# A new order of tasks within a pair, on all five queues of an attention and channel-mix kernel

## The chip, the cores and the metric

The kernel runs on one core of one Trainium2 chip. The metric is device time in microseconds, from launch to end, as the median of several executions. The core has TensorE (PE; its weight loads are listed as PEld), VectorE (DVE), ScalarE (ACT), GpSimd (POOL) and a sync queue (SP) that issues DMAs. Each of them works through its own list of instructions in order, and they meet at semaphores.

## What is computed

One transformer-like layer on x of 8 x 1024 x 256, with 16 heads of 64:

```
h   = layernorm(x)
q,k,v = h @ Wq, h @ Wk, h @ Wv                     # per head, 64 wide
s   = q k^T / 8 + bias[clip(j - i + 16, 0, 32)]    # causal
a   = softmax(s) @ v                               # 16 heads side by side: 1024
x2  = x + layernorm(a @ Wp + bp)
n   = layernorm(x2);  p = n shifted down by one token
r   = sigmoid((mu_r n + (1 - mu_r) p) @ W_r^T)
k   = relu((mu_k n + (1 - mu_k) p) @ W_k^T)^2
out = x2 + layernorm(r * (k @ W_v^T))
```

## The kernel before

**Tiling.** The unit of work is a pair: two heads of one batch element, 8 x 8 = 64 pairs, n = 0 to 63 (n = 2m + par, so par is 0 in an even pair, and `at` is n mod 8). While attention runs for pair n, the second pass over the row maxima ("next") is made for pair n+1, q, k and v are projected ("qkv") for pair n+2, the block of 128 tokens n+10 is loaded, normalised and transposed ("xt"), and the tail of the layer runs for older blocks: the output projection ("proj") for block n-8, the mix ("mix") for n-9, the last matmul and gate ("ffn") for n-10. Not all parts run in all pairs: "xt" up to n = 53, "proj" from 8, "mix" from 9, "ffn" from 10. The tails of the last eight blocks are done after the last pair, in code of its own.

**Numbers as a pair of fp16.** Matmul operands are split: a high part (fp16 copy, made by ACT) and a low part (difference, made by VectorE or GpSimd), and three products are summed. So nearly each result of TensorE in PSUM is read first by ACT and then by VectorE before its bank is free.

**The tasks of a pair.** Attention of a pair goes through 12 tiles of scores (`TILES`), keys by queries, up to 128 x 512 for both heads. `score(t)` writes one of two score banks, `add_bias` (VectorE) adds the position bias to tiles on the diagonal, `exponential` and `high_probs` (ACT) follow, then `low_probs` on VectorE, or on GpSimd for tiles 4, 6, 7, 8, 10. Score t needs the bank of score t-2, that is low part t-2, or exponential t-2 for a tile of GpSimd, which copies out to SBUF. `weigh_values(k)`, k = 0 to 3 (tasks o0 to o3), multiplies probabilities and values of two blocks of 128 tokens; 2 and 3 of a pair run in the next pair. `outputs(k)` divides by the sums, into o_stage, and `store_chunk` writes o_stage to o_scratch in DRAM, in two halves. `fill(0)` to `fill(8)` write raw scores of the next pair to max_ps and `maxima` (VectorE) reduces them; `transpose_maxima(0)` and `(1)` turn the results over, also in max_ps, ACT's `shift` scales them to shift_row, and the sync queue's `load_shift` spreads them to shift_all, which enters the scores as one more product (L633). fill(0) waits for shift 1, because it writes what shift 1 reads; score 4 waits for the second half of shift_all.

**Banks.** All other tasks of TensorE share two PSUM banks, misc0 and misc1. The list `TASKS` gives their order in a pair, with the bank of each. `opened` (L551) lets a task wait until the task before it on the same bank is freed by its last reader (`freed`, L343). The order is written out by hand once for each engine, in `body` of each block, and must agree with `TASKS`.

**The sync queue.** `held` makes it wait for a semaphore, and everything behind it waits too. load_outputs (o_cur, 512 KB, for the output projection) waits until all chunks it reads are stored; load_head (xh, 128 KB) for the last transpose of a block; load_values (v_pair, 516 KB) for the values of a block of heads, which par 1 asks for in the pair in which the last of them, v1, is projected; load_residual (x_res, 128 KB) for GpSimd's last residual; store_out for GpSimd's `final`.

**GpSimd.** `head`, `residual_norm`, `final` and `residual` are layer norms (`normalise`, L382 to L399, a chain of tiny steps and one of 256 columns), each behind VectorE's `statistics`.

**The lists.** The old order of TensorE in a pair is: ffn, fill 0, score 1, o2, q0, q1, fill 1, scores 2 and 3, o0, o3, ot0, score 4, fill 2, o1, ot1, fill 3, scores 5 and 6, k0, first transpose of the maxima, k1, fill 4, scores 7 and 8, fill 5, v0, fill 6, score 9, x2t, proj, fill 7, score 10, xt, v1, fill 8, rk, score 11, score 0 of the next pair, second transpose of the maxima.

## Time and profile before

| | us |
|---|---|
| median of 3 executions (2397.15 to 2404.86) | 2400.41 |
| profiled execution | 2395.8 |
| its span, first to last instruction | 2394.0 |
| TensorE busy | 2221.1 |
| VectorE busy | 2043.0 |
| ACT busy | 1681.4 |
| GpSimd busy | 1498.1 |

The busy times are of the whole span. A pair takes some 35 us; the first 80 us go to loads and to the splitting of the weights, and the last 100 us to the tails of the last eight blocks. The 1.8 us between the profiled execution's time and its span lie around the instructions. The granted clock of TensorE is 0.985 of its full 2.4 GHz on average.

### The profile page before, as it was taken

What the parts mean: (1) busy time and instruction counts of PE and PEld (TensorE: products, weight loads), DVE (VectorE), ACT (ScalarE), POOL (GpSimd) and SP (SyncE); (2) the same over time, 40 slices, a digit from 0 to 9 for tenths busy, and PEclk for the clock granted to TensorE, in tenths of its full rate; (3) what the DMA queues carried; (4) which work ended last, traced back from release to release, by engine and by line L of the source; (5) the groups of instructions that cost most, each with busy time, mean ns of one, the idle gap of its engine ahead of it and who ended that gap; (6) DMA issues with size and microseconds to landing.
All of it is one profiled execution on the core that took longest, in us unless ns stands there. A gap on an engine that the chain in (4) does not pass through costs nothing.

```text
span 2394.0 us, 75663 instructions
## 1 busy us (share of the span) xinstructions
PE 2221.1 (93%) x30080; PEld 1486.8 (62%) x30080; DVE 2043.0 (85%) x3985; ACT 1681.4 (70%) x2526; POOL 1498.1 (63%) x2594
## 2 busy tenths in 40 slices
PE   3788889999999999999999999999999999999885
PEld 1455556666666666666666666666666666666664
DVE  6788878988888898888888988889898898988856
ACT  2577767777777776777777777777777777777743
POOL 2244335667776766767767777677677767565752
PEclk9999999999999999999999999999999999999997
DMA  6011111122122112212112211211221221121230
GB/s 166 28 41 42 40 48 51 39 68 64 52 65 64 57 42 68 62 50 68 55 39 68 64 57 59 64 57 42 68 63 50 67 62 52 40 64 59 62 108 21
DMA packets 182416, 139.81 MB, mean 58 GB/s; under 512 B 10416, under 2 KB 173104, under 8 KB 182064
## 3 DMA queue, kind: packets, MB, share of 16 engines
q1 hardware_dynamic: 182064, 134.98, 19.1%
q8 instruction: 238, 3.90, 0.7%
q14 instruction: 114, 0.93, 0.1%
HBM read 57.81 MB, written 43.06 MB: 42 GB/s over the span
## 4 chain that ended last, share of the span: by engine, by line
PE 77%; DVE 8%; DMA 6%; SPq 3%; ACT 3%; issue 2%; POOL 1%; DVEq 0%; POOLq 0%; ACTq 0%
PE score_ps L629 13%; PE misc L585 11%; PE misc L600 7%; PE max_ps L651 6%; PE misc L712 6%; PE misc L694 6%; DMA xh<-x 5%; PE misc L696 5%; PE misc L695 5%; PE score_ps L633 4%; PE misc L732 2%; PE misc L706 2%; PE misc L735 2%; PE max_ps L660 2%; DVE probs L1226 1%
## 5 line engine op out<-in xcount | busy, mean ns | idle before, releaser
L1670 POOL TENSOR_TENSOR probs<-probs_f,probs 128x1024 f16<-128x1024 f32 (+1 forms) x320 | 616.7, 1936 | 344.9 <-DVE x_mv L1192 194.5
L1242 DVE TENSOR_REDUCE row_max<-max_ps 128x2 f32<-128x1024 f32 (+2 forms) x640 | 633.0, 1006 | 29.9 <-PE max_ps L660 15.2
L977 ACT ACTIVATE score_ps<-score_ps,score_unit 128x1024 f32<-128x1024 f32 (+3 forms) x448 | 347.9, 777 | 197.9 <-DVE score_ps L1258 150.4
L694 PE MATMUL misc<-v_pair,probs 128*128 128x65 f16 x4608 | 445.3, 195 | 11.3 <-DVE q_lo L1201 7.8
L694 PEld LDWEIGHTS misc<-v_pair,probs 128*128 128x128 f16 x4608 | 418.9, 97 | 46.5 <-issue 36.7
L695 PE MATMUL misc<-v_pair,probs 128*128 128x64 f16 x4608 | 443.9, 194 | 0.0
L696 PE MATMUL misc<-v_pair,probs 128*128 128x65 f16 x4608 | 443.2, 194 | 0.0
L696 PEld LDWEIGHTS misc<-v_pair,probs 128*128 128x128 f16 x4608 | 421.5, 98 | 0.0
L695 PEld LDWEIGHTS misc<-v_pair,probs 128*128 128x128 f16 x4608 | 421.3, 98 | 0.0
L1226 DVE TENSOR_TENSOR probs<-score_ps,probs 128x1024 f16<-128x1024 f32 (+3 forms) x448 | 373.7, 834 | 46.1 <-ACT probs L995 43.4
L585 PE MATMUL misc<-xT,w_split 128*128 128x512 f16 x1536 | 369.6, 385 | 25.6 <-DVE o_stage L1270 16.5
L977 ACT ACTIVATE probs_f<-score_ps,score_unit 128x1024 f32<-128x1024 f32 (+1 forms) x320 | 328.1, 1025 | 54.1 <-PE score_ps L633 36.0
L995 ACT CAST probs<-score_ps 128x1024 f16<-128x1024 f32 (+3 forms) x448 | 317.3, 708 | 12.5
L995 ACT CAST probs<-probs_f 128x1024 f16<-128x1024 f32 (+1 forms) x320 | 307.3, 960 | 4.2
L629 PE MATMUL score_ps<-q_hi,k_hi 64*128 64x512 f16 (+3 forms) x1536 | 253.5, 325 | 37.0 <-DVE probs L1226 35.4
L1258 DVE TENSOR_TENSOR score_ps<-score_ps,bandT 128x288 f32<-128x288 f32 (+2 forms) x576 | 236.0, 420 | 44.5 <-PE score_ps L633 43.9
L585 PEld LDWEIGHTS misc<-xT,w_split 128*128 128x128 f16 x1536 | 140.7, 99 | 203.9 <-issue 44.1
L651 PE MATMUL max_ps<-k_hi,q_hi 64*128 64x512 f16 (+3 forms) x1536 | 225.4, 330 | 35.6 <-DVE row_max L1242 21.7
L633 PE MATMUL score_ps<-shift_all,shift_unit 64*128 64x512 f16 (+3 forms) x1536 | 252.2, 324 | 0.0
L629 PE MATMUL score_ps<-q_lo,k_hi 64*128 64x512 f16 (+3 forms) x1536 | 252.0, 323 | 0.0
L629 PE MATMUL score_ps<-q_hi,k_lo 64*128 64x512 f16 (+3 forms) x1536 | 252.0, 323 | 0.0
L600 PE MATMUL misc<-w_split,xT 128*128 128x256 f16 x1536 | 193.3, 277 | 0.0
(181 smaller groups left out, 4062.8 us busy)
## 6 DMA issues: line engine op xcount, KB each, us to landing
v_pair<-v_calc SPq DMA_DIRECT2D x64, 516.0 KB, 3.7
o_scratch<-o_stage SPq DMA_DIRECT2D x128, 256.0 KB, 2.5
o_cur<-o_scratch SPq DMA_DIRECT2D x56, 512.0 KB, 4.6
xh<-x SPq DMA_DIRECT2D x56, 128.0 KB, 4.1
x_res<-x SPq DMA_DIRECT2D x56, 128.0 KB, 2.1
out<-out_sb SPq DMA_DIRECT2D x56, 128.0 KB, 1.7
shift_all<-shift_row SPq DMA_DIRECT2D x256, 1.0 KB
probs<-wqkv SPq DMA_DIRECT2D x1, 3072.0 KB, 13.2
```

Of the source, the lines that this page charges most:

```text
L585: last = pe.matmul(bank[:], w_split[:, w, which, k, bass.ds(pair, P)], xT[:, a, k, bass.ds(ring + half * 512, 512)], start=step == 0, stop ...
L600: last = pe.matmul(bank[:, i * 2 * P:(i + 1) * 2 * P], xT[:, a, k, bass.ds(ring + (first + i) * P, P)], w_split[:, w, 2, k, bass.ds(pairs, ...
L629: pe.matmul(tile[:, h, 0:width], k_part[rows, ring, keys], q_part[rows, ring, cols], start=step == 0, stop=False)
L651: last = pe.matmul(max_ps[:, h, col:col + width], qk_hi[0][rows, ring, i * P:(i + 1) * P], qk_hi[1][rows, ring, key:key + width], start=Tr ...
L694: pe.matmul(bank[:, at:at + D + 1], high, v_high, start=j == 0, stop=False)
L695: pe.matmul(bank[:, at:at + D], high, v_low, start=False, stop=False)
L696: last = pe.matmul(bank[:, at:at + D + 1], low, v_high, start=False, stop=j == i)
L977: nc.scalar.activation(dst, score_ps[t % 2][:, :, 0:width], ACT.Exp, scale=score_unit[:]).then_inc(exp_done, 1)
L995: nc.scalar.copy(dst, src).then_inc(hi_done, 1)
L1226: dve.tensor_tensor(low, score_ps[t % 2][:, :, 0:width], high, ALU.subtract).then_inc(lo_done_dve, 1)
L1242: last = dve.tensor_reduce(dst[:, :, i % 4:i % 4 + 1], max_ps[:, :, col:col + width], AX.X, ALU.max)
L1670: pool.tensor_tensor(low, copy_of(par + ahead, t)[:, 0:2 * width], high, ALU.subtract).then_inc(lo_done_pool, 1)
```

## The change

The same tasks are done with the same instructions and the same waits, in another order, on all engines and on the sync queue, and with other banks for some tasks. The new order of TensorE in a pair is: fill 0, score 1, o2, q0, score 2, fill 1, score 3, o3, score 4, fill 2, q1, score 5, fill 3, score 6, k0, first transpose of the maxima, ot0, fill 4, score 7, ffn, score 8, fill 5, o0, v0, fill 6, v1, scores 9 and 10, fill 7, o1, k1, ot1, fill 8, score 11, score 0 of the next pair, x2t, proj, rk, second transpose of the maxima, xt. After the last pair, o2 and o3 come ahead of ffn. On the sync queue the load of the next block and of shift_all go to the beginning, the stores to the end. GpSimd does low parts 6 and 7 ahead of the norm of the residual, and 8 and 10 ahead of `final`. ACT and VectorE follow TensorE's order.

```diff
--- before.py
+++ after.py
-TASKS = [("ffn", 0, "ffn"), ("o2", 1, "prev"), ("q0", 0, "qkv"), ("q1", 1, "qkv"), ("o0", 0, "att"),
-         ("o3", 1, "prev"), ("ot0", 0, "proj"), ("o1", 1, "att"), ("ot1", 0, "proj"), ("k0", 1, "qkv"),
-         ("k1", 0, "qkv"), ("v0", 1, "qkv"), ("x2t", 0, "mix"), ("proj", 1, "proj"), ("xt", 1, "xt"),
-         ("v1", 0, "qkv"), ("rk", 1, "mix")]
+TASKS = [("o2", 0, "prev"), ("q0", 1, "qkv"), ("o3", 0, "prev"), ("q1", 0, "qkv"), ("k0", 0, "qkv"),
+         ("ot0", 1, "proj"), ("ffn", 0, "ffn"), ("o0", 1, "att"), ("v0", 0, "qkv"), ("v1", 1, "qkv"),
+         ("o1", 0, "att"), ("k1", 1, "qkv"), ("ot1", 0, "proj"), ("x2t", 1, "mix"), ("proj", 0, "proj"),
+         ("rk", 1, "mix"), ("xt", 0, "xt")]
...
@@ sync queue @@
+                    if has["att"]:
+                        load_shift(m, par, 0, 1)
+                    if has["xt"] and (not isinstance(m, int) or n > -LEAD):
+                        load_head(n + HEAD_LEAD)
                     if has["proj"]:
                         load_outputs(n, at)
-                    if has["xt"] and (not isinstance(m, int) or n > -LEAD):
-                        load_head(n + HEAD_LEAD)
-                    if has["att"]:
-                        load_shift(m, par, 0, 1)
+                    if has["next"] and par == 0:
+                        load_values(m, par)
+                    if has["next"]:
+                        load_shift(m, par, 1, 0)
+                    if has["next"] and par == 1:
+                        load_values(m, par)
                     if has["proj"]:
                         load_residual(n - PROJ_LAG)
-                    if has["next"] and par == 0:
-                        load_values(m, par)
-                    if has["att"]:
-                        store_chunk(m, par, 0, 0, at)
-                    if has["next"]:
-                        load_shift(m, par, 1, 0)
+                    if has["prev"]:
+                        store_chunk(m, par, 1, 1, at)
                     if has["ffn"]:
                         store_out(n - FFN_LAG)
-                    if has["next"] and par == 1:
-                        load_values(m, par)
-                    if has["prev"]:
-                        store_chunk(m, par, 1, 1, at)
+                    if has["att"]:
+                        store_chunk(m, par, 0, 0, at)
...
@@ TensorE, the end of a pair @@
-                    if has["next"]:
-                        fill(m, par, 7, at)
-                    if has["att"]:
-                        score(m, par, 0, 10, at)
+                    if has["mix"]:
+                        tail_gate_and_key(n, span)
+                    if has["next"]:
+                        transpose_maxima(1, n)
                     if has["xt"]:
                         head_transpose(n, span)
-                    if has["qkv"]:
-                        project_v("v1", n, 4 * par + 2, pair // 2 * 2 * P, ring, span)
-                    if has["next"]:
-                        fill(m, par, 8, at)
-                    if has["mix"]:
-                        tail_gate_and_key(n, span)
-                    if has["att"]:
-                        score(m, par, 0, 11, at)
-                    if has["next"]:
-                        score(m, par, 1, 0, at)
-                        transpose_maxima(1, n)
...
@@ ACT, the end of a pair @@
+                    if has["att"]:
+                        exponential(m, par, 0, 11)
+                        high_probs(m, par, 0, 10)
+                    if has["next"]:
+                        exponential(m, par, 1, 0)
+                    if has["att"]:
+                        high_probs(m, par, 0, 11)
+                    if has["next"]:
+                        high_probs(m, par, 1, 0)
+                        shift(m, par, 1, 1)
                     if has["xt"]:
                         col = (m + HEAD_LEAD // 2) % (RING // P // 2) * 2 * P
                         col = (col if isinstance(m, int) else act.snap(col)) + par * P
                         head_high(n + HEAD_LEAD, col, misc[BANK["xt"]])
...
@@ VectorE, the beginning of a pair @@
-                    if has["ffn"]:
-                        gated(n)
+                    if has["att"]:
+                        add_bias(m, par, 0, 1, at)
                     if has["next"]:
                         maxima(m, par, 1, 0)
                     if has["att"]:
-                        add_bias(m, par, 0, 1, at)
                         low_probs(m, par, 0, 0)
+                        low_probs(m, par, 0, 1)
                     if has["prev"]:
                         outputs(2, m, par, 1)
+                    if has["att"]:
+                        add_bias(m, par, 0, 2, at)
+                    if has["next"]:
+                        maxima(m, par, 1, 1)
+                    if has["att"]:
+                        add_bias(m, par, 0, 3, at)
+                        low_probs(m, par, 0, 2)
+                    if has["qkv"]:
+                        low_part("q0", m, par, at)
+                    if has["prev"]:
+                        outputs(3, m, par, 1)
                     if has["xt"]:
                         statistics("xh", xh, n + LEAD, xh_in, 16 * (n + LEAD + 1))
...
@@ GpSimd @@
                         low_probs(m, par, 0, 4)
+                        low_probs(m, par, 0, 6)
+                        low_probs(m, par, 0, 7)
                     if has["mix"]:
                         residual_norm(n, par)
                     if has["att"]:
-                        low_probs(m, par, 0, 6)
-                        low_probs(m, par, 0, 7)
+                        low_probs(m, par, 0, 8)
+                        low_probs(m, par, 0, 10)
                     if has["ffn"]:
                         final(n, par)
-                    if has["att"]:
-                        low_probs(m, par, 0, 8)
-                        low_probs(m, par, 0, 10)
                     if has["proj"]:
                         residual(n, par)
```

On VectorE the last steps of a pair are now, in this order: mix, maxima 8, the output projection's result, join_maxima, low part 11, the statistics of y, head_low. On ACT the gate of rk follows head_high.

## Rows read from the trace of the kernel before

**Rows 1.** The page, busy us and share of the span by engine.
```profile
PE 2221.1 (93%) x30080; PEld 1486.8 (62%) x30080; DVE 2043.0 (85%) x3985; ACT 1681.4 (70%) x2526; POOL 1498.1 (63%) x2594
```
**Rows 2.** Timeline of TensorE: start us, us; pair starts, second transposes of the maxima.
```profile
78.82 0.33 PE L671 MATMUL max_ps<-ident,row_max 128*128 128x128 f32 x1 [1.13 <-DVE row_max L1249]
...
339.69 0.33 PE L671 MATMUL max_ps<-ident,row_max 128*128 128x128 f32 x1 [0.87 <-DVE row_max L1249]
...
411.28 1.04 PE L743 MATMUL misc<-wv_sb,k_act 128*128 128x256 f32 x4
...
1959.11 1.04 PE L743 MATMUL misc<-wv_sb,k_act 128*128 128x256 f32 x4
...
2264.69 1.04 PE L743 MATMUL misc<-wv_sb,k_act 128*128 128x256 f32 x4
```
**Rows 3.** Windows: stretch, its length, busy us by engine, clock, DMA share.
```profile
1009.89:1043.95 34.06, 34.03 (x471) 22.97 (x471) 31.30 (x60) 25.90 (x40) 25.04 (x46) 1.00 0.15 45
1043.95:1080.51 36.56, 34.30 (x471) 22.93 (x471) 31.20 (x60) 25.91 (x40) 25.03 (x46) 1.00 0.24 71
```
**Rows 4.** The list of waits: us in total, times, longest.
```profile
DVE xh_bn L1188 <- DMA xh<-x: 44.4, 30, 3.4
...
PE score_ps L629 <- DVE probs L1226: 35.4, 37, 2.9
...
DVE o_stage L1270 <- DMA o_scratch<-o_stage: 26.4, 28, 2.2
```
**Rows 5.** Timelines of an even pair: sync queue, VectorE, TensorE; brackets: idle before.
```profile
1043.67 0.67 SPq L433 DMA_DIRECT2D v_pair<-v_calc  x1
...
1045.19 1.08 SPq L453 DMA_DIRECT2D o_cur<-o_scratch  x1
1046.37 0.81 SPq L463 DMA_DIRECT2D xh<-x  x1
...
1051.92 0.43 DVE L1188 BATCH_NORM_STATS2 xh_bn<-xh 128x6 f32<-128x256 f32 x1 [2.94 <-DMA xh<-x]
...
1053.56 0.23 PE L629 MATMUL score_ps<-q_hi,k_hi 64*128 64x128 f16 x2 [1.94 <-DVE probs L1226]
```
**Rows 6.** Timeline of GpSimd: first steps of residual, head and final; two low parts.
```profile
1012.32 0.19 POOL L382 TENSOR_SCALAR y_half_var<-y_mv 128x1 f32<-128x1 f32 x1
...
1018.06 0.19 POOL L382 TENSOR_SCALAR xh_half_var<-xh_mv 128x1 f32<-128x1 f32 x1
...
1037.44 0.19 POOL L382 TENSOR_SCALAR z_half_var<-z_mv 128x1 f32<-128x1 f32 x1
...
1043.05 3.24 POOL L1670 TENSOR_TENSOR probs<-probs_f,probs 128x1024 f16<-128x1024 f32 x2
```
**Rows 7.** Us from issue to landing: o_cur's median on the page; tile xh.
```profile
o_cur<-o_scratch SPq DMA_DIRECT2D x56, 512.0 KB, 4.6
...
DMA to landing us min/median/max: 2.0/4.1/6.7
```
**Rows 8.** VectorE: a group (busy us, mean ns) of 400:2200; timeline, odd pair's waits.
```profile
L1226 DVE TENSOR_TENSOR probs<-score_ps,probs 128x1024 f16<-128x1024 f32 x102 | 124.4, 1220 | 18.5 <-ACT probs L995 18.4
...
1015.02 0.43 DVE L1188 BATCH_NORM_STATS2 xh_bn<-xh 128x6 f32<-128x256 f32 x1 [0.23 <-DMA xh<-x]
...
1043.04 0.43 DVE L1258 TENSOR_TENSOR score_ps<-score_ps,bandT 128x256 f32<-128x256 f32 x1 [0.22 <-PE score_ps L633]
```
**Rows 9.** Timelines, odd pair: first transpose of the maxima, ACT's shift, xt.
```profile
1028.13 0.27 PE L671 MATMUL max_ps<-ident,row_max 128*128 128x128 f32 x1
...
1028.44 0.36 ACT L959 ACTIVATE shift_row<-max_ps,shift_bias 8x128 f16<-8x128 f32 x1 [0.24 <-PE max_ps L671]
...
1038.54 0.44 PE L571 MATMUL misc<-ident,xh 128*128 128x128 f32 x2
```
**Rows 10.** Timeline of TensorE: the first fill in an early and in the odd pair.
```profile
209.49 0.61 PE L651 MATMUL max_ps<-k_hi,q_hi 64*128 64x384 f16 x4 [0.83 <-ACT shift_row L959]
...
1010.88 0.40 PE L651 MATMUL max_ps<-k_hi,q_hi 64*128 64x384 f16 x4
```

More of the change, by code:

```diff
@@ L795, in body @@
                         transpose_maxima(0, n)
-                    if has["qkv"]:
-                        project_qk("k1", n, pair * P, ring, span)
+                    if has["proj"]:
+                        tail_transpose("ot0", n, span)
                     if has["next"]:
@@ L804, in body @@
                         fill(m, par, 5, at)
+                    if has["att"]:
+                        weigh_values(0, m, par, 0, span)
                     if has["qkv"]:
```

174 lines of the change are left out of this document (84 added, 90 removed).

## The prediction

> **What bounds the kernel now.** I read the busy shares first: TensorE is at work for 93% of the span, VectorE for 85%, ACT and GpSimd have room [rows 1]. Then the pair times. From the matmuls of tail_value, which open each pair, the 44 pairs n=10 to 53 take (1959.11-411.28)/44 = 35.18 us, the nine pairs 54 to 62, which load no block, (2264.69-1959.11)/9 = 33.95 us, and from one second transpose of the maxima to another the eight pairs 0 to 7 take (339.69-78.82)/8 = 32.61 us [rows 2]. Then two neighbours by stretches: an odd pair lasts 34.06 us with TensorE busy 34.03 and VectorE 31.30; the even pair after it has the same work and lasts 36.56 [rows 3]. So 34.06 us is what TensorE's instructions cost with no wait, and on average 1.12 us of a pair is waiting. The list of waits names it: VectorE waited 44.4 us for the load of xh, 30 times, and 26.4 us for the store of o_stage; TensorE waited 35.4 us for VectorE's low parts of the probabilities [rows 4]. The even pair shows the chain. The sync queue issues v_pair, o_cur and only then xh; xh's statistics stand early on VectorE, wait 2.94 us, and TensorE's score 3 waits 1.94 us behind them [rows 5].
>
> **The change part by part.** No instruction is added or removed, so the floor of 34.06 us stays. What moves is who waits.
>
> Sync queue. load_head goes from behind load_outputs to before it, its statistics on VectorE from sixth to twelfth place. v0 and v1 are projected at 19 to 22 us of a pair, not at 22 and 29, so an odd pair's 516 KB load of v_pair is issued near 24 us, no longer in one burst with the next pair's loads. Both causes of the 2.94 us wait go. The store of chunk (1,1) is issued within the pair, 10 us or more before outputs(2) asks for it, so the 26.4 us go as well. Moved past on this queue: each load_shift(0,1), load_head and load_outputs now stands behind the previous pair's store_out and store_chunk(0,0).
>
> GpSimd. Low parts 6 and 7 go ahead of residual_norm, 8 and 10 ahead of final. In the odd pair final and its addition took 5.6 us, the two low parts 3.2, residual 5.7 [rows 6], and head, the same steps without the addition, 4.9; with the other three low parts and residual_norm the sum is some 31.1 us, so there is room in 34. But final now ends about 3.2 us into the next pair, and store_out holds the sync queue until then. Issue of what is behind it takes 2.3 us (the two pieces of shift_all end it at 5.5), then comes load_head at 5.5 to 6, then o_cur. How long the shift pieces take to land no row shows: between nothing and the 4.6 us of o_cur, 512 KB; I take 2.0, the least that the 128 KB of xh took, as the row nearest in size [rows 7]. That is 7.5, and score 4 starts at 8.4. xh alone landed in 2.0 us at the least, in 4.1 in the middle when o_cur was ahead of it [rows 7]: it is there at 7.5 to 9.6, and its statistics come up at 9.0. o_cur is there by 12 and is read at 14.8.
>
> Here I lean on two rows: xh needs 4.1 us behind o_cur and 2.0 without. The Trainium skill ("DMA: Bandwidth & Descriptors", section on queues, rings and completion order) says that descriptors on an engine are taken in ring order but that completion is not first-in first-out per issuer; were xh slowed by an o_cur issued behind it as by one ahead, the sum would lose what the second rival says, 26 us. The same page (anatomy of one DMA) gives some 2.0 us fixed for a small transfer, an estimate that would put the shift pieces at 7.5.
>
> TensorE and VectorE. I laid the new order out with the steps of the odd pair, whose TensorE had no wait [rows 3], start to start from its timeline: fill0 0.31, score 1 0.76, o2 2.0, q0 1.35, o3 2.7, score 4 0.97 and so on to x2t at 28.3, proj, rk, the second transpose at 33.4 and xt. VectorE's 46 steps sum to 32.1 us (34.06 less 1.93 us of waits in that pair, eight of them, of which the rows show the first and the last; a low part of 1024 columns is 1.22 us busy) [rows 8]. Following both lists, each place where TensorE needs VectorE or ACT comes out in time, but with little to spare: score 3 needs low part 1 at 4.8 and stands at 5.2; o3 needs o2's bank at 5.4, stands at 5.5; q1 9.1 against 9.5; k0 12.7 against 13.0; score 7 needs low part 5 at 15.3, stands at 15.4; score 8 needs exponential 6 at 17.0, stands at 17.2; fill5 18.2 against 18.1; ot1 26.1 against 26.2; rk 31.5 against 31.5. VectorE must idle some 1.6 us at the end of a pair, because head_low, now its last step, follows xt, TensorE's last; that fits its 1.9 us of room.
>
> Two new waits. (a) The second transpose of the maxima had tail_value (1 us) between it and fill0; now only xt. fill0 needs the transpose (0.27), ACT's shift (0.36) and two handovers of 0.05: 0.73 us from its start, against the transpose's step of 0.16 and xt's at most 0.44 [rows 9]. That leaves 0.1 to 0.3 us; I take 0.24. Behind fill0 waits all of TensorE. (b) The first transpose had k1 (1.3 us) behind it, now ot0 (0.5 to 0.6): 0.1 us. So a steady pair is 34.06+0.24+0.10 = 34.40 us.
>
> Sum, against the profiled execution's 2395.8 us. Pairs 10 to 53: 44 x (35.18-34.40) = -34.3. Pairs 54 to 62 were nearly free of waits and get (a) whole, since xt is not there to cover it, though it is also not in the work: 9 x (34.40-33.95) = +4. Pairs 0 to 7: neither engine is full there; the new order ends in ACT's run of exponential 11, high 10, exponential 0, high 11, high 0, shift. Laid out the same way it gives 31.6 against 32.6: -8. TensorE's waits bundle there at the pair's end, 1.8 and 1.3 us. Pairs 8 and 9: between -5 and 0, I take -3. End: final(63) comes 3.3 us later, with it the store and the first loads of the last block, and the work after the last pair starts with transposes of these; the second half's loads come earlier: between 0 and +4, I take +2. Start: 0, within 1. In all -39.3, so 2356.5; the median of the three runs is 4.6 above the profiled one, so **2361 us**.
>
> On the clock: in the early pairs the first fill behind two waits of 1.25 and 0.83 us took 0.61 us where the odd pair's took 0.40, which I read as the lower of the two levels, 1.2 GHz [rows 10]. Waits of the same size, placed elsewhere, may do that or not; this is inside the bounds of the early term. The Trainium skill ("TensorE: Matmul & The Clock Gate", what is actually happening) says idleness brings the clock down; it neither adds to nor takes from the sum.
>
> **The rivals.** (1) Slower: a new loop closes, final on GpSimd, store_out, load_shift, score 4, high 6, three low parts, residual_norm, final. From final to the last issue 2.3, landing L, score 4 to the end of high 6 9.8, GpSimd from there 18.5: 30.6+L. With L=2.0 it is 32.6 and hidden; it decides above L=3.8. At 5 us, somewhat over o_cur's 4.6, a pair takes 35.65: +21 for 44 pairs, +15 for nine, -8 -3 +2: 2428 by the median. For it: the 256 KB store stands directly ahead. Against: 128 KB landed in 2.0 [rows 7]. (2) Partly: the joints with 0.1 us of room slip, or xh lands at 9.6 and VectorE waits 0.6 in every pair. A pair of 35.0 loses 26 us of the gain: 2387. For it: VectorE has only 1.9 us of room and spends 1.6 at one place. (3) Nothing: the waits move and each pair still takes 35.2, while early and late terms cancel: 2400. Against: the odd pairs show that the old order runs at the floor as soon as its load is in time [rows 3]. (4) Better: shift hides behind xt and the early pairs gain 1.5 us each: 2345. That the change does not do what it says, with xh still late, is case (2) at 0.6, and (3) at 1.1 us.
>
> **How the numbers follow.** Forecast 0.58, its own range 2350 to 2375. Rival 4 0.06, rival 2 0.18, rival 3 0.06, rival 1 0.12. A measurement here can tell about 0.3%, 7 us. Faster: 0.58+0.06+0.18 = 0.82; same 0.06; slower 0.12. The range leaves out rival 1 and the far end of rival 4: 2340 to 2396.
>
> **What would show it.** After the change the wait of VectorE for xh and for the store of o_stage is gone from the list; even and odd pairs last the same, near 34.4; the wait of fill0 for shift_row grows to some 0.2 us a pair; the sync queue waits for out_sb until 3 us into a pair; v_pair is issued at 8 and 24 us. It would be wrong if score 4 waited for shift_all, if xh's statistics still waited, or if TensorE waited for low parts 5 and exponential 6 in each pair.

## The result, and the profile after

The changed kernel takes 2328.26 us (median of 4 executions, 2327.67 to 2331.38) against 2398.78 (2396.84 to 2404.86) of the kernel before on the same chip: ratio 0.9704, 95% interval 0.9684 to 0.9725. That is 70.5 us less. The forecast was 39 less, 2361, and the time lies below its range.

One correction first, since much hangs on it. My list of the new order says that fill 0 stands ahead of score 1. The changed code has it the other way round: score 1 comes first, then fill 0. I misread a hunk of the diff which the excerpt above leaves out. The trace shows the true order. Timeline of TensorE, the start of a pair (start us, us):

```profile
1013.87 0.27 PE L671 MATMUL max_ps<-ident,row_max 128*128 128x128 f32 x1
1013.98 0.38 PE L571 MATMUL misc<-ident,xh 128*128 128x128 f32 x2
1014.30 0.34 PE L629 MATMUL score_ps<-q_hi,k_hi 64*128 64x384 f16 x2
...
1014.96 0.38 PE L651 MATMUL max_ps<-k_hi,q_hi 64*128 64x384 f16 x4
```

Between the second transpose (L671) and fill 0 (L651) lie xt, 0.32 us, and the whole of score 1, 0.66 us.

The profiled execution took 2327.67 us, its span is 2325.9. The page's busy times, to be held against [rows 1], and the windows of an odd and an even pair, against [rows 3]:

```profile
PE 2203.7 (95%) x30080; PEld 1487.8 (64%) x30080; DVE 2028.7 (87%) x3985; ACT 1669.1 (72%) x2526; POOL 1494.3 (64%) x2594
```
```profile
980.09:1013.87 33.78, 33.77 (x472) 23.02 (x471) 30.92 (x61) 25.67 (x39) 24.97 (x45) 1.00 0.21 61
1047.87:1081.66 33.79, 33.78 (x473) 23.03 (x471) 31.06 (x61) 25.67 (x39) 24.83 (x45) 1.00 0.20 60
```

Even and odd pairs are now alike, TensorE is never idle in either, and both are shorter than the 34.06 us that I had called the floor. The same number of matmuls keeps TensorE busy for 17 us less.

The waits of pairs 10 to 53 (us 405 to 1893; total, times, longest), to be held against [rows 4]:

```profile
DVE xh_bn L1192 <- DMA xh<-x: 6.1, 9, 1.3
...
PE max_ps L651 <- DVE row_max L1246: 0.6, 4, 0.2
...
PE score_ps L629 <- DVE probs L1230: 0.5, 2, 0.4
```

VectorE's wait for xh is 6.1 us, where the kernel before had 43.1 in the same pairs (44.4 in its whole span); the wait for the store of o_stage, 18.6 us there, is gone from the list; TensorE's own waits sum to 1 us. The page's DMA section shows why: the median from issue to landing of xh is 2.2 us, where it was 4.1 [rows 7], although o_cur is now issued right behind it.

```profile
o_cur<-o_scratch SPq DMA_DIRECT2D x56, 512.0 KB, 4.1
xh<-x SPq DMA_DIRECT2D x56, 128.0 KB, 2.2
```

The sync queue in the even pair that begins at 1047.87 (timeline, start us, us) stands against [rows 5]:

```profile
1051.76 0.34 SPq L467 DMA_DIRECT2D out<-out_sb  x1
1052.25 0.37 SPq L444 DMA_DIRECT2D o_scratch<-o_stage  x1
1052.71 1.21 SPq L423 DMA_DIRECT2D shift_all<-shift_row  x2
1054.01 0.40 SPq L463 DMA_DIRECT2D xh<-x  x1
1054.56 0.63 SPq L453 DMA_DIRECT2D o_cur<-o_scratch  x1
...
1072.55 0.67 SPq L433 DMA_DIRECT2D v_pair<-v_calc  x1
```

The last pair's store is released 3.9 us into the pair, xh is issued at 6.1, o_cur at 6.7, v_pair at 24.7: within 1 us of what I had laid out (3.2, 5.5 to 6, 24).

Where the 68.1 us between the two spans lie, by the times of the second transposes (the start, and all pairs up to 62) and what follows the last:

| stretch | before, us | after, us | difference | forecast |
|---|---|---|---|---|
| start to the first of them | 78.8 | 77.4 | -1.4 | 0 |
| pairs 0 to 7, each | 32.61 | 32.43 | -1.4 in all | -8 |
| pairs 8 and 9 | 35.92, 35.51 | 34.90, 33.62 | -2.9 | -3 |
| pairs 10 to 53, each | 35.18 | 33.83 | -59.3 | -34.3 |
| pairs 54 to 62, each | 33.95 | 33.31 | -5.8 | +4 |
| the rest | 129.5 | 132.1 | +2.6 | +2 |

### The profile page after: what moved, and what is told of

Same layout as the page of the kernel before. It is cut to its first block, busy times and chain, and to the rows that moved or that the text cites. A ratio compares the mean times of both kernels' runs of the same rounds, so it can differ in the third digit from the quotient of the medians.

```text
span 2325.9 us, 75663 instructions
## 1 busy us (share of the span) xinstructions
PE 2203.7 (95%) x30080; PEld 1487.8 (64%) x30080; DVE 2028.7 (87%) x3985; ACT 1669.1 (72%) x2526; POOL 1494.3 (64%) x2594
## 4 chain that ended last, share of the span: by engine, by line
PE 84%; DVE 5%; ACT 3%; POOL 3%; issue 2%; DMA 1%; SPq 0%; POOLq 0%; DVEq 0%; ACTq 0%
PE score_ps L629 16%; PE misc L585 14%; PE misc L600 7%; PE misc L694 7%; PE max_ps L651 6%; PE misc L712 6%; PE misc L695 5%; PE misc L696 5%; PE score_ps L633 5%; PE misc L743 2%; PE misc L735 2%; PE misc L732 2%; PE max_ps L660 2%; PE misc L706 2%; POOL probs L1676 2%
## 5 line engine op out<-in xcount | busy, mean ns | idle before, releaser
L982 ACT ACTIVATE score_ps<-score_ps,score_unit 128x1024 f32<-128x1024 f32 (+3 forms) x448 | 352.7, 787 | 206.6 <-DVE score_ps L1262 204.4
L585 PE MATMUL misc<-xT,w_split 128*128 128x512 f16 x1536 | 379.3, 384 | 12.1 <-DVE w_split L1372 6.6
L1230 DVE TENSOR_TENSOR probs<-score_ps,probs 128x1024 f16<-128x1024 f32 (+3 forms) x448 | 367.2, 831 | 26.2 <-ACT probs L1000 26.1
L1000 ACT CAST probs<-score_ps 128x1024 f16<-128x1024 f32 (+3 forms) x448 | 311.4, 713 | 10.2
L585 PEld LDWEIGHTS misc<-xT,w_split 128*128 128x128 f16 x1536 | 131.9, 98 | 170.4 <-DVE q_lo L1205 26.4
L651 PE MATMUL max_ps<-k_hi,q_hi 64*128 64x512 f16 (+3 forms) x1536 | 222.5, 327 | 16.7 <-DVE row_max L1246 7.4
```

What stands on the lines that cost most here:

```text
L585: last = pe.matmul(bank[:], w_split[:, w, which, k, bass.ds(pair, P)], xT[:, a, k, bass.ds(ring + half * 512, 512)], start=step == 0, stop ...
L651: last = pe.matmul(max_ps[:, h, col:col + width], qk_hi[0][rows, ring, i * P:(i + 1) * P], qk_hi[1][rows, ring, key:key + width], start=Tr ...
L982: nc.scalar.activation(dst, score_ps[t % 2][:, :, 0:width], ACT.Exp, scale=score_unit[:]).then_inc(exp_done, 1)
L1000: nc.scalar.copy(dst, src).then_inc(hi_done, 1)
L1230: dve.tensor_tensor(low, score_ps[t % 2][:, :, 0:width], high, ALU.subtract).then_inc(lo_done_dve, 1)
```

## The experiments

The theory after the result: the waits went as forecast, by the sync queue's order; what is better than forecast is my misread joint and a TensorE order that itself costs less. The rivals: (i) VectorE's later statistics, or GpSimd's order, carry the gain; (ii) the floor did not fall, but waits of both kernels were hidden in it. The ratios below are to the kernel before on the same chip. The pair times are means over pairs 10 to 53, and the waits are of us 800 to 1400, some 17 pairs, unless said otherwise.

**From the kernel before towards the changed one.** First only the two loads change places on the sync queue:

```diff
-                    if has["proj"]:
-                        load_outputs(n, at)
                     if has["xt"] and (not isinstance(m, int) or n > -LEAD):
                         load_head(n + HEAD_LEAD)
+                    if has["proj"]:
+                        load_outputs(n, at)
```

> The kernel before, with one edit: on the sync queue the load of xh is issued ahead of the load of o_cur. Theory (late load): what cost the old order 1.12 us a pair was xh landing behind 512 KB of o_cur; it lands some 2 us earlier, VectorE's wait for it falls from 44 us to under 15, TensorE's waits for low parts with it, pairs 10 to 53 average 34.2 to 34.5 instead of 35.18: 2360 to 2370. Rival (tight joints of the old order): the pairs stay at 35.0 or more and the time at 2390 or more, whatever the load does.

Measured: 2355.85 us, ratio 0.9824 (0.9798 to 0.985). A pair takes 34.29; the wait for xh is down to one of 0.2 us. What is left of waits is o_stage's:

```profile
DVE o_stage L1270 <- DMA o_scratch<-o_stage: 8.2, 7, 2.4
```

Two lines exchanged on one queue bring 42 of the 70 us. Then VectorE's statistics alone, and both together:

```diff
-                    if has["xt"]:
-                        statistics("xh", xh, n + LEAD, xh_in, 16 * (n + LEAD + 1))
...
                     if has["att"]:
                         low_probs(m, par, 0, 3)
+                    if has["xt"]:
+                        statistics("xh", xh, n + LEAD, xh_in, 16 * (n + LEAD + 1))
```

> The kernel before, with one edit: VectorE takes the statistics of xh behind low part 3 instead of behind outputs(2), some 7 us later. Late load: VectorE's wait for xh is gone and pairs average 34.3 to 34.6; GpSimd's head starts later and may hand part of it on: 2362 to 2375. Rival (tight joints): 2390 or more.

> The kernel before, with both edits: xh loaded ahead of o_cur and its statistics behind low part 3. Late load: no wait for xh; what is left is the wait for the store of o_stage (26 us in all): pairs 34.1 to 34.5, 2355 to 2368. Rival: 2390 or more. If it is no better than each edit alone, one of them was enough.

Measured: 2430.04 (1.013, 1.0106 to 1.0153) and 2434.63 us (1.0146, 1.012 to 1.0173). Both are slower than before, at 35.92 and 36.00 us a pair. So the later statistics are no half of the cure in the old order; they harm it. To see whether only the stores stood in the way, the third kernel got one edit more, as in the change: the store of chunk (1,1) ahead of the values and of store_out.

```diff
+                    if has["prev"]:
+                        store_chunk(m, par, 1, 1, at)
+                    if has["next"] and par == 1:
+                        load_values(m, par)
                     if has["ffn"]:
                         store_out(n - FFN_LAG)
-                    if has["next"] and par == 1:
-                        load_values(m, par)
-                    if has["prev"]:
-                        store_chunk(m, par, 1, 1, at)
```

> As the one with both edits, and on the sync queue the store of chunk (1,1) and par 1's load of v_pair stand ahead of store_out. All waits for DMAs that the trace of before names are gone; the engines keep the old order. If the old order costs 34.06 us a pair with no wait, the average is 34.06 to 34.15 and the time 2398.8 - 44 x 1.1 = 2350, between 2344 and 2356. What is left to the new kernel's 2328 is then due to the order on the engines, not to the queue. Rival (the queue alone is enough): 2335 or less.

Measured: 2391.93 us (0.9978, 0.9965 to 0.9991), 35.2 us in even and odd pairs alike: still 1.1 above the floor, though no wait for xh or o_stage is left. The list names another engine, in nearly every pair:

```profile
POOL xh_half_var L382 <- issue: 72.3, 17, 4.3
...
ACT probs_f L977 <- POOL probs L1670: 26.6, 17, 1.6
```

In the old order GpSimd does head (its first step is xh_half_var), which needs the statistics, ahead of low part 4. With late statistics it stands idle for 4.3 us in front of head in each pair, the low parts and the residual's norm come late, and ACT waits 1.6 us for a buffer of probabilities. The list says "issue", which names no releaser, but VectorE ends the statistics at 1022.57 and head begins at 1022.73. I took all that for a matter of head's place, and put head behind low part 4 on top of it:

```diff
-                    if has["xt"]:
-                        head(n)
                     if has["att"]:
                         low_probs(m, par, 0, 4)
+                    if has["xt"]:
+                        head(n)
```

> As the one with late statistics, xh first and the stores (35.2 us a pair), and on GpSimd head stands behind low part 4. If the late statistics cost 1.1 us a pair because head waits for them in front of low part 4, and GpSimd's list becomes the loop, pairs fall to 34.1 to 34.5: 2345 to 2365. Rival (VectorE's order itself is what costs): 35.2, 2392.

Measured: 2501.06 us (1.0421, 1.0403 to 1.0439), 37.57 a pair, and the wait of x2t has grown:

```profile
POOL probs L1670 <- ACT probs L995: 103.6, 16, 6.8
PEld misc L725 <- POOL y L399: 42.0, 16, 2.9
```

That head's place is the cause is refuted. What the loop is can be read from the chain of work that ended last, in the kernel with the statistics late and head ahead of low part 4 (us 1007 to 1043, one pair of 35.1): GpSimd's idle 4.25 us, head, low part 4, the residual's norm, the next low part; then ACT's exponential into the buffer which that one frees; then VectorE's last steps of the pair, TensorE's second transpose and first tasks of the next pair; and, behind those, the late statistics again. With head behind low part 4 the chain takes the same steps of GpSimd in the other order, and the idle time in front of them is 6.6 us, now for ACT's high part 4. Without late statistics (the next kernel) head follows the norm before it with no wait. So in the old order late statistics close a loop through GpSimd.

The other way is to leave the statistics alone and take both edits of the sync queue, the loads' and the stores':

> The kernel before, with the sync queue alone changed: xh ahead of o_cur, and the store of chunk (1,1) and par 1's v_pair ahead of store_out; VectorE's order stays. With xh first alone the odd pairs took 34.06, the even ones 34.52. If what is left there is the wait for the store of o_stage, all pairs take 34.06 to 34.15 and the time is 2356 - 22 x 0.46 = 2345. Then the old order's floor is 34.06, and the 0.28 us to the new kernel's 33.78 belongs to TensorE's order. Rival (another wait hides there): 34.3 or more, 2353 or more.

Measured: 2338.41 us (0.9745, 0.9729 to 0.9761). Every pair from 10 to 53 takes 34.05 to 34.33, on average 34.061, with no wait for o_stage and one of 0.8 us for xh. This tells two things apart. The sync queue's order alone, with no engine touched, gives 59 us of the 70; how that divides between the store of chunk (1,1) and the load of v_pair, which moved together, no run tells. And 34.06 is the floor of the old order of TensorE, so the changed kernel's 33.78 is another floor and not a wait removed from the even pairs.

**From the changed kernel back.** The two loads exchanged again, o_cur ahead of xh:

```diff
-                    if has["xt"] and (not isinstance(m, int) or n > -LEAD):
-                        load_head(n + HEAD_LEAD)
                     if has["proj"]:
                         load_outputs(n, at)
+                    if has["xt"] and (not isinstance(m, int) or n > -LEAD):
+                        load_head(n + HEAD_LEAD)
```

> The changed kernel, with one part undone: load_outputs stands ahead of load_head again. Late load: xh lands 4.1 us or more after an issue 6 us into the pair, 1 us or more behind the place of its statistics; VectorE has 1.6 us of room, so pairs take 34.0 to 34.8 instead of 33.8: 2335 to 2370. Rival (the later place of the statistics is what removed the wait, the queue order is idle): 2328, unchanged.

Measured: 2382.68 us (0.9943, 0.9928 to 0.9959); a pair takes 34.98. The wait for xh is back and TensorE's behind it, as in [rows 4]:

```profile
DVE xh_bn L1192 <- DMA xh<-x: 32.6, 17, 4.0
...
PE score_ps L629 <- DVE probs L1230: 17.5, 14, 3.1
```

Next the pieces of shift_all behind both loads; this opens the first rival's loop on purpose:

```diff
-                    if has["att"]:
-                        load_shift(m, par, 0, 1)
                     if has["xt"] and (not isinstance(m, int) or n > -LEAD):
                         load_head(n + HEAD_LEAD)
                     if has["proj"]:
                         load_outputs(n, at)
+                    if has["att"]:
+                        load_shift(m, par, 0, 1)
```

> The changed kernel, with load_shift(0,1) behind load_head and load_outputs, that is behind 640 KB. This is the loop that I named as the slower rival, with a long landing: the pieces of shift_all land with or behind o_cur, 10.5 us or later into a pair, score 4 stands at 8.8: pairs of 35 to 36.5, 2380 to 2440. Rival (small pieces do not queue behind large loads): their own issue is 1.2 us later, landing near 9.8: pairs of 33.8 to 34.6, 2328 to 2365.

Measured: 2396.17 us (0.9984, 0.9967 to 1.0002), 35.15 a pair. All of the change's gain is gone with one move:

```profile
PE score_ps L629 <- DMA shift_all<-shift_row: 21.9, 18, 2.7
```

So the rival's mechanism is real, 1.2 us of waiting a pair, and what kept it out is that the shift pieces stand first. The chain that ended last (us 1000 to 1072) goes once a pair through just the steps that I had named: final, the store, the queue's issues, 2.4 to 3.2 us of landing, score 4, TensorE's next tasks, high 6, low parts, residual_norm, final. Then the values of par 1 back into one burst, behind the stores at the end of the pair:

```diff
-                    if has["next"] and par == 1:
-                        load_values(m, par)
...
                     if has["att"]:
                         store_chunk(m, par, 0, 0, at)
+                    if has["next"] and par == 1:
+                        load_values(m, par)
```

> The changed kernel, with par 1's load of v_pair issued behind the stores, at the beginning of the next pair as before the change; the projection of the values stays in the middle. If that burst matters beside the place of xh's statistics: 516 KB ahead of shift_all and xh in even pairs, score 4 or the statistics late by 0.5 to 2 us there: 2340 to 2375. If not (the rest of the order gives room enough): 2328 to 2332.

Measured, in two executions: 2361.2 us (0.9844, 0.9821 to 0.9866). Even pairs take 35.06, odd ones 33.82, the alternation of [rows 3]; VectorE waits for xh again (17.8 us in 11 pairs) and score 4 for shift_all (4.7 in 9). This is the part which the earlier v1 makes possible. The statistics put back to the sixth place:

```diff
+                    if has["xt"]:
+                        statistics("xh", xh, n + LEAD, xh_in, 16 * (n + LEAD + 1))
                     if has["att"]:
                         add_bias(m, par, 0, 2, at)
                     if has["next"]:
                         maxima(m, par, 1, 1)
```

> The changed kernel, with the statistics of xh behind outputs(2), in sixth place, as before. Late load: xh is issued 6 us into a pair and needs 2 us, the place comes at 5.3: VectorE waits some 2.8 us in each pair, of which TensorE feels 1 to 2: pairs of 34.8 to 35.8, 2375 to 2420. Rival (the load is early enough): 2328.

Measured, in two executions: 2574.4 us (1.0747, 1.0722 to 1.0772), 39.3 a pair, the granted clock 0.947 on average:

```profile
DVE xh_bn L1192 <- DMA xh<-x: 60.2, 16, 5.0
PE score_ps L629 <- DVE probs L1230: 59.0, 16, 4.9
```

The direction was expected, the size was far off: xh, held by the previous pair's store, lands 3.8 us too late for that place on average and 5.0 at most, and nearly all of it falls on TensorE. Of the 5.5 us that a pair is longer than the changed kernel's, 3.6 are idle time of TensorE; the other 1.9 are longer busy time of the same matmuls, at a clock of 0.94 for 1.00. Early statistics suit the old lists of the engines, with the queue's order as it was or mended (34.06 a pair), and late ones the new lists; neither bears the other's. Last of the five queues, final back ahead of low parts 8 and 10 on GpSimd:

```diff
+                    if has["ffn"]:
+                        final(n, par)
                     if has["att"]:
                         low_probs(m, par, 0, 8)
                         low_probs(m, par, 0, 10)
-                    if has["ffn"]:
-                        final(n, par)
```

> The changed kernel, with final ahead of low parts 8 and 10 on GpSimd, as before. final ends 3.3 us earlier, so the sync queue is freed at the end of a pair and not 3 us into the next. If the queue has room, the pairs stay at 33.78 and only the end gains, 1 to 3 us: 2326. If the sync queue's late start costs anything in the pairs, they get shorter. If low part 8 or 10 becomes late, they get longer, 34 or more.

Measured: 2369.12 us (0.9876, 0.9858 to 0.9893), 34.53 a pair. o2, at the beginning of a pair, waits for low part 10:

```profile
PE misc L694 <- POOL probs L1676: 12.7, 17, 1.0
```

**TensorE's order.** The order that I had priced, fill 0 ahead of score 1:

```diff
-                    if has["att"]:
-                        score(m, par, 0, 1, at)
                     if has["next"]:
...
                         fill(m, par, 0, at)
+                    if has["att"]:
+                        score(m, par, 0, 1, at)
```

> The changed kernel, with fill 0 ahead of score 1 on TensorE, which is the order that my prediction was worked out for; the change has score 1 ahead. My term (a): fill 0 waits 0.1 to 0.3 us for shift 1 in each pair: pairs of 33.9 to 34.1, and 6 to 19 us in all, 2334 to 2347. Rival (the handover is hidden anyway): 2328.

Measured: 2363.33 us (0.9865, 0.985 to 0.9879), 35 us above the changed kernel. A pair takes 34.18, one of 54 to 62 33.94, one of 0 to 7 33.63, and the wait is the one described:

```profile
PE max_ps L651 <- ACT shift_row L964: 5.5, 17, 0.3
```

Against the changed kernel that is 0.35 a pair where I took 0.24, 15 us in 44 pairs, and 0.62 in each of the last nine, 6 us. Another 10 us are in the first eight pairs (below) and 2 in pairs 8 and 9. The last 4 lie ahead of the first second transpose, at 81.5 us where it was 77.4; as that time lies between 75.4 and 81.5 in all kernels here, I don't count them. Then whether the new floor has to do with which tiles are neighbours. Fill 8, a tile of 64 rows, put between x2t and proj, both of 128 rows:

```diff
-                    if has["next"]:
-                        fill(m, par, 8, at)
...
                         tail_residual_transpose(n, span)
+                    if has["next"]:
+                        fill(m, par, 8, at)
                     if has["proj"]:
```

> The changed kernel, with fill 8 moved on TensorE from behind ot1 to between x2t and proj; VectorE has the time for it. Theory (steps depend on their neighbours): a step of 64-row tiles costs 0.10 us more when a 128-row one follows, and this adds one such change of form in each pair: 33.88 instead of 33.78, 2332 to 2338. Rival (a task costs the same wherever it stands, and the pair got shorter for another reason): pairs of 33.78, 2328.

Measured: 2348.97 us (0.9807, 0.9791 to 0.9823); every pair takes 34.24, 0.45 more. Timelines of TensorE, x2t (L725) to the start of proj (L712), first of the changed kernel, then of this one:

```profile
1009.22 0.44 PE L725 MATMUL misc<-ident,y 128*128 128x128 f32 x2
1009.50 2.78 PE L712 MATMUL misc<-wp_split,oT 128*128 128x256 f16 x24
```
```profile
1050.49 0.44 PE L725 MATMUL misc<-ident,y 128*128 128x128 f32 x2
1050.86 0.39 PE L651 MATMUL max_ps<-k_hi,q_hi 64*128 64x512 f16 x2
...
1051.28 0.50 PE L712 MATMUL misc<-wp_split,oT 128*128 128x256 f16 x3
```

The step of a task is the time from its start to the next one's. x2t's step is 0.28 us ahead of proj and 0.37 ahead of a fill; fill 8's step is 0.32 ahead of a score and 0.42 ahead of proj. Each passage from one form of tile to the other costs 0.09 to 0.10 us with the same instructions. That explains 0.19 of the 0.45; the rest is score 11, which has lost the fill ahead of it and now waits for low part 9 in every pair (0.2 us each); with that wait in it the step of ot1, ahead of score 11, grew by 0.23. My expectation had only the first. The Trainium skill ("TensorEngine Tiling (Array Packing)", key properties) says that changing the tiling mode drains TensorE; this trace agrees, and gives the price here.

**Towards a better one.** The two stores at the end of the queue's list exchanged, so that the half of o_stage goes ahead of the one which waits for final:

```diff
+                    if has["att"]:
+                        store_chunk(m, par, 0, 0, at)
                     if has["ffn"]:
                         store_out(n - FFN_LAG)
-                    if has["att"]:
-                        store_chunk(m, par, 0, 0, at)
```

> The changed kernel, with store_chunk(0,0) ahead of store_out on the sync queue. The pairs stay at 33.78. From the second transpose of the maxima of pair 62 to the end the changed kernel takes 132.1 us, the one before 129.5; if that is the late store of the last pair's first half behind final(63), it falls to 129.5 to 131 and the time to 2326 or so. Rival (the end is bound by the order on TensorE): 132.1, no change.

Measured: 2323.34 us (2319.56 to 2323.53), ratio 0.9682 (0.9666 to 0.9698). The changed kernel, measured again on another chip than this one, gave 2328.06 (2327.25 to 2329.04), ratio 0.9703 (0.9688 to 0.9719):

> The changed kernel once more, unedited, on the chip of this group, beside the others: 2328 and 33.8 us a pair. It says how much of 2328 against 2323 is the chip and how much the moved store.

The two intervals touch, the two sets of times do not. In the profiled executions the pairs are nearly the same (33.79), the last second transpose comes 3.0 us earlier and what follows it is 5.1 shorter. Windows of what follows it, of the changed kernel and of this one; the first of the last three numbers is the granted clock:

```profile
2193.79:2325.88 132.09, 95.32 (x935) 76.87 (x933) 75.79 (x249) 54.77 (x108) 51.98 (x100) 0.86 0.19 66
```
```profile
2190.76:2317.76 127.00, 89.70 (x935) 72.73 (x933) 75.44 (x249) 54.72 (x108) 52.00 (x100) 0.93 0.19 66
```

The idle time of TensorE, which the moved store was to shorten, is no shorter, 36.8 and 37.3 us. The same 935 matmuls are busy 5.6 us less, at a clock of 0.93 in place of 0.86; busy time by missing clock (TensorE's busy time times one less the clock, summed over windows of 1 us) is 4.5 us for 11.1, and 10.2 in the changed kernel's second profile. So the expected mechanism did not show, and in the profiled execution the gain at the end is the clock.

That execution was 3.8 us below its kernel's other three. Their mean clocks over the whole span are 0.987, 0.988 and 0.988, against 0.984 to 0.987 in the eight of the changed kernel; a clock lower by 0.002 over 2320 us makes some 4.6 us, so the clock may account for all of the gain. But the two executions at 0.987, one of each kernel, took 2323.4 and 2328.4. So the kernel measures 5 us, 0.2%, faster, in four executions, on another chip than at least four of the changed kernel's eight; why is not shown.

On top of this, v0 and v1 side by side, fill 6 behind them, and on VectorE the maxima of fill 6 between the low parts of both:

```diff
+                    if has["qkv"]:
+                        project_v("v1", n, 4 * par + 2, pair // 2 * 2 * P, ring, span)
                     if has["next"]:
                         fill(m, par, 6, at)
-                    if has["qkv"]:
-                        project_v("v1", n, 4 * par + 2, pair // 2 * 2 * P, ring, span)
```

> The changed kernel with store_chunk(0,0) ahead of store_out, and v1 directly behind v0 on TensorE, fill 6 behind both (VectorE takes maxima 6 between the low parts of v0 and v1). Theory (a step costs 0.10 more at a change of form): one change less, pairs of 33.6 to 33.7 instead of 33.78, 2314 to 2320, if VectorE keeps up. Rival (VectorE, with maxima 6 later by 1.4 us, becomes the loop): 33.9 or more, 2328 or more.

Measured: 2354.49 us (0.9807, 0.979 to 0.9825), 34.29 a pair. The tenth that a saved passage should bring is lost in new waits, VectorE's for the fill and TensorE's for VectorE:

```profile
DVE row_max L1246 <- PE max_ps L660: 10.0, 18, 0.6
...
PE max_ps L651 <- DVE row_max L1246: 4.3, 18, 0.2
```

## Why the prediction was right and where it was wrong

**Which step failed.** The sum's price of a steady pair, 34.06+0.24+0.10 = 34.40 us: measured were 33.83. All three terms were too high, the floor by 0.28, (a) by 0.24 and (b) by 0.07. Beside it failed the last nine pairs, put at the same price (+4 forecast, -5.8 measured), and the early ones (-8 forecast, -1.4 measured). Each is taken up below.

**The waits: right.** Both causes were named. The first is shown from either side: one exchange of loads brings 42 us to the old kernel and takes 54 from the new. The second, the values in a burst, is shown from the new kernel's side, where it takes 33; the old kernel got that edit only together with the store of chunk (1,1). With o_cur behind it xh lands in 2.2 us, and in 3.6 with the two exchanged again, so the second rival, which rested on xh being as slow as before or on slipping joints, fell. That the later place of the statistics helps is true of the new lists alone; in the old ones it costs 32 us. The first rival did not happen, but one move on the queue brings it about: the shift pieces two places further back. Its sum of 30.6 us plus landing was fit for the question. In two pairs of that kernel it took 5.3 and 6.0 us from final's end to the landing, with two more issues ahead of the pieces, 9.9 to the end of high 6 (I had 9.8) and 19.1 on GpSimd from there (18.5): 34.3 and 35.0, where the mean of 44 pairs is 35.15. That the even and odd pairs become alike, that the queue is free 3 to 4 us into a pair, and that final may end in the next pair came out as forecast.

**"No instruction is added or removed, so the floor of 34.06 us stays": wrong,** by 0.28 us a pair. The step times hang on the neighbour. Timeline of the odd pair before, its x2t, proj and rk, against the changed kernel's:

```profile
1034.60 0.44 PE L725 MATMUL misc<-ident,y 128*128 128x128 f32 x2
1035.08 2.78 PE L712 MATMUL misc<-wp_split,oT 128*128 128x256 f16 x24
1037.79 0.39 PE L651 MATMUL max_ps<-k_hi,q_hi 64*128 64x512 f16 x2
...
1040.64 1.13 PE L732 MATMUL misc<-wr_sb,mixed 128*128 128x256 f32 x4
...
1042.60 0.23 PE L629 MATMUL score_ps<-q_hi,k_hi 64*128 64x128 f16 x2
```
```profile
1009.50 2.78 PE L712 MATMUL misc<-wp_split,oT 128*128 128x256 f16 x24
1012.12 1.03 PE L732 MATMUL misc<-wr_sb,mixed 128*128 128x256 f32 x4
...
1013.87 0.27 PE L671 MATMUL max_ps<-ident,row_max 128*128 128x128 f32 x1
```

Start to start, proj took 2.71 us ahead of a fill and takes 2.62 ahead of rk; rk took 1.96 ahead of a score and takes 1.75 ahead of the transpose; x2t went from 0.48 to 0.28. Those three make 0.50; steps that became dearer elsewhere (fill 0 from 0.31 to 0.44, ffn from 0.99 to 1.07) give part of it back. Since both orders pass nine times from one form to the other in a pair, it is not the count but which steps stand at the passages: rk, with its fp32 operands, loses 0.21 there, others 0.1. The 0.20 of x2t is something else: proj's bank in the old order was v0's, whose low part VectorE ended at 1034.93, 0.15 ahead of proj's start. That it was a short wait, which the row of the window with 34.03 busy of 34.06 hides because ends of matmuls are modelled, is argued and not shown.

**Term (a), 0.24 us for fill 0: wrong by misreading.** In the real change score 1 covers it. For the order that I had in mind the mechanism was right and the size too small: 0.35 in a steady pair and 0.62 in a late one. In the early pairs, where it is 1.2 us, most of it by the clock, I had not charged it at all. That this order came out at 2363, two us from my 2361, is luck, errors which cancel: its steady pairs were 0.2 cheaper than my 34.40, its early ones 2 us dearer than my 31.6.

**Term (b), 0.10 us for ot0 behind the first transpose: too large.** The step of fill 4 is 0.35 us against 0.32: 0.03. With (a) away, (b) smaller and the floor lower, my 34.40 becomes 34.40-0.24-0.07-0.28 = 33.81; measured were 33.83 on average. That is 25 us of the miss in pairs 10 to 53 and 10 in 54 to 62.

**Pairs 0 to 7: -8 forecast, -1.4 measured.** Windows of these eight pairs, the kernel before and after it the changed one:

```profile
78.82:339.69 260.87, 221.84 (x3205) 138.94 (x3205) 213.85 (x366) 188.44 (x265) 104.88 (x113) 0.97 0.13 36
```
```profile
77.40:336.87 259.47, 227.81 (x3204) 137.59 (x3205) 215.36 (x365) 189.25 (x266) 104.29 (x113) 0.96 0.13 37
```

TensorE waits 7.4 us less (31.7 against 39.0, length less busy), which is what I had laid out. But the same matmuls are busy for 6.0 us more, at a granted clock of 0.96 for 0.97. Going through the stretch in windows of 1 us, the clock falls to its lower level, 0.5 or 1.2 GHz, four times in the kernel before and six times in the changed one, for 3 to 4 us each; busy time by missing clock sums to 6.6 and 10.0 us. So 3.4 of the 6.0 us are the clock. The other 2.6 belong to the order of TensorE: busy time less that missing to the clock is 213.8 to 215.3 us in these pairs in the seven kernels with the old order, 217.7 to 218.2 in the nine with score 1 ahead of fill 0, and 215.6 in the one with fill 0 first. So 2.2 of the 2.6 come with the place of score 1; whether they are dearer steps or a wait which the modelled ends hide is not shown.

In the changed kernel the clock falls five of the six times within 2 us of a second transpose, where this kernel bundles its wait. One of these, and windows of 2 us behind two such transposes, at 206.90 and at 238.88:

```profile
238.88 0.33 PE L671 MATMUL max_ps<-ident,row_max 128*128 128x128 f32 x1 [1.90 <-DVE row_max L1253]
...
240.12 0.49 PE L633 MATMUL score_ps<-shift_all,shift_unit 64*128 64x384 f16 x2
240.40 0.64 PE L651 MATMUL max_ps<-k_hi,q_hi 64*128 64x384 f16 x4
```
```profile
208.00:210.00 2.00, 1.78 (x44) 1.30 (x41) 1.28 (x8) 0.51 (x3) 0.00 (x0) 1.00 0.00 1
...
240.00:242.00 2.00, 2.00 (x30) 1.38 (x27) 1.48 (x4) 2.00 (x5) 0.00 (x0) 0.54 0.03 9
```

Both transposes had waited 1.9 us; behind the one the clock stayed at 1.00, behind the other it fell and fill 0 took 0.64 us for 0.38. Behind three of the eight such transposes (at 77.40, 206.90 and 271.28) it did not fall. That such waits may be paid again in slower matmuls I had put down as "inside the bounds"; the 3.4 us are nearly half of the 7.4 that were to be had.

That they come from the bundling is argued and not shown: the changed kernel's second profile has its six falls in the same places and 11.1 us, but kernels with the old order of TensorE, whose waits there are 0.8 to 1.25 us, have from three falls and 4.9 us to nine and 15.3.

The kernel with fill 0 first is clear of that spread. There a second wait stands behind the first, the clock falls once in each of the eight pairs, for 3 to 4 us in three of them and for 7 in five,

```profile
81.48:350.50 269.02, 236.00 (x3204) 144.80 (x3205) 215.86 (x365) 189.56 (x266) 104.56 (x113) 0.92 0.13 36
```

and busy time by missing clock is 20.1 us, 10 more than in the changed kernel. Its first eight pairs are 9.6 us longer, 8.2 of it busy time. The Trainium skill ("TensorE: Matmul & The Clock Gate", what is actually happening) says that idleness brings the clock down; the falls behind the waits agree, and the three waits of the same 1.9 us with no fall show that such a wait alone does not decide it.

**The small terms.** Pairs 8 and 9 came out (-2.9 for -3). The end came out by luck (+2.6 for +2): I had charged it to later stores and loads, but TensorE idles 36.8 us there as before (36.9), and busy time by missing clock is 11.1 us for 9.0. The start gave 1.4 for 0, less than it differs between kernels here. I added 4.6 us for the median over the profiled execution; it was 0.6, another 4 of the miss. In all: 25 + 9.8 - 6.6 + 1.4 - 0.6 - 0.1 + 4.0 = 32.9 of the 32.7 between 2361 and 2328.3.

**Still open:** the 0.20 us of x2t; how the 17 us that the stores' edit adds to the loads' divide between its two parts; how much of the 5 us of the exchanged stores is the clock; and whether the bundled wait or chance made the early pairs' clock lower.

## What to carry to other kernels

Before an order of tasks is rewritten, look at what each queue holds back: here two exchanges on one DMA queue carried 59 of 70 us, and each list's place for a step (a load, its statistics, a norm) suited only the other lists' places for the same step. A floor read from a wait-free stretch is the floor of that order and no other, so price each step with its neighbours; and trace an order from the code line by line, since one joint read the wrong way round was worth some 32 us. Where joints have 0.1 to 0.2 us of room, each tenth gained at one place was lost several times over at the next.

## What the runs showed of the hardware

- A TensorE step costs some 0.10 us more when its tile has the other number of rows than the next one's: x2t 0.28 and 0.37, a fill 0.32 and 0.42, score 1 0.66 ahead of a fill and 0.76 ahead of o2, with fp32 operands 0.21 (rk, 1.75 and 1.96).
- Two 1 KB pieces behind 640 KB of loads on the same queue made their reader wait 1.2 us in each pair, up to 2.7; 128 KB behind 512 KB took 4.1 us to land in the kernel before and 3.6 in the changed kernel with the loads exchanged, ahead of them 2.2.
- A wait of TensorE of 1.9 us came with 3 to 4 us at half the clock at five of the changed kernel's early pairs and with none at three others of the same size; with a second wait behind it (fill 0 first) the clock fell once in each of eight pairs, for up to 7 us. Two kernels that differ by two exchanged stores had 0.86 and 0.93 of the clock in what followed their last second transpose (132.1 and 127.0 us).
